# A GRU's input projection by Strassen's seven half products in place of eight, with the step loops written out

## The reference

```python
def cell(h, x):                        # 1024 steps in sequence, B = 4, D = 1024, float32
    gi = x @ W_ih + b_ih               # the projection: needs no h
    gh = h @ W_hh + b_hh               # the recurrence
    i_r, i_z, i_n = split(gi, 3); h_r, h_z, h_n = split(gh, 3)
    r = sigmoid(i_r + h_r); z = sigmoid(i_z + h_z)
    n = tanh(i_n + r * h_n)
    return (1 - z) * n + z * h
hs = scan(cell, cond, x)               # [4, 1024, 1024]
# mixture of experts on hs: the router takes x/|x| @ router_w, softmax, the best 2 of 8,
# their weights normalised
out = x + sum_e combine[:, e] * (hs @ Wa[e] @ Wb[e])     # rank 128
```

## Time and profile before

| what | value |
|---|---|
| median of 3 runs | 9792.21 us (9789.74 to 9792.78) |
| the profiled execution, its own time | 9795.94 us |
| its span, first to last instruction | 9794.1 us |
| mean granted TensorE clock | 0.998 |
| PE busy | 9705.0 us, 99% |
| DVE busy | 5534.7 us, 57% |
| ACT busy | 1224.2 us, 12% |
| POOL busy | 488.3 us, 5% |

### The profile page before, as it was taken

The page is one execution under the profiler, slowest core; times in us unless marked ns, Lnnn a source line. Parts: engine busy times, 40 slices in busy tenths (PEclk is TensorE's granted clock), DMA queues, the critical chain, the costliest instruction groups (busy, mean ns, idle before and its releaser), DMA issues.

```text
span 9794.1 us, 528922 instructions
## 1 busy us (share of the span) xinstructions
PE 9705.0 (99%) x230296; PEld 6479.3 (66%) x230296; DVE 5534.7 (57%) x29395; ACT 1224.2 (12%) x4788; POOL 488.3 (5%) x1142
## 2 busy tenths in 40 slices
PE   7999999999999999999999999999999999999999
PEld 4666666667666676666767666676676766767676
DVE  5555555555555555555555555555555555555664
ACT  2111111111111111111111111111111111111111
POOL 1000000000000000000000000000000000000100
PEclk9999999999999999999999999999999999999999
DMA  7121222212222122222222222222222222222343
GB/s 171 40 46 46 47 50 44 47 42 48 49 46 50 39 49 64 67 59 60 59 66 64 63 60 60 65 64 63 64 54 68 64 64 64 58 62 61 86 101 91
DMA packets 1421900, 603.63 MB, mean 62 GB/s; under 512 B 852816, under 2 KB 1373520, under 8 KB 1419536
## 3 DMA queue, kind: packets, MB, share of 16 engines
q1 hardware_dynamic: 1395216, 491.58, 21.6%
q0 software_dynamic: 24336, 77.98, 3.5%
HBM read 436.35 MB, written 159.72 MB: 61 GB/s over the span
## 4 chain that ended last, share of the span: by engine, by line
PE 97%; DVE 1%; DMA 1%; issue 0%; SPq 0%; ACT 0%; DVEq 0%
PE gh_ps L1114 80%; PE gi_ps L1136 13%; PE y_ps L1174 1%; PE y_ps L1187 1%; PE route_ps L1147 1%; DMA w_ih_tile<-in_L_cond_W_ih 1%; DVE gh L839 0%; PE gh_ps L1258 0%; PE gi_ps L1187 0%; PE gi_ps L1174 0%; DVE gh_sum L845 0%; SPq L353 0%; PE gi_ps L1244 0%; SPq L358 0%; ACT gate L1037 0%
## 5 line engine op out<-in xcount | busy, mean ns | idle before, releaser
L1114 PE MATMUL gh_ps<-w_hh_parts,h_parts 128*12 128x288 bf16 (+1 forms) x196608 | 8363.3, 326 | 33.3 <-DVE h_parts L890 13.5
L1114 PEld LDWEIGHTS gh_ps<-w_hh_parts,h_parts 128*12 128x12 bf16 x196608 | 5396.9, 88 | 2674.3 <-issue 98.4
L839 DVE STREAM_TRANSPOSE gh<-gh_ps 128x288 f32<-128x288 f32 (+1 forms) x2048 | 1193.3, 583 | 2525.9 <-PE gh_ps L1114 2522.5
L1136 PE MATMUL gi_ps<-x_t,w_ih_tile 128*32 128x256 f32 x24576 | 1682.9, 381 | 43.3 <-DMA w_ih_tile<-in_L_cond_W_ih 43.2
L1037 ACT ACTIVATE gate<-pre 128x24 f32<-128x24 f32 (+1 forms) x2048 | 471.1, 230 | 7303.1 <-DVE pre L852 7303.1
L1136 PEld LDWEIGHTS gi_ps<-x_t,w_ih_tile 128*32 128x32 f32 x24576 | 813.2, 111 | 561.4 <-DMA w_ih_tile<-in_L_cond_W_ih 48.6
L860 DVE TENSOR_TENSOR r_cand<-h_cand,gate 128x12 f32<-128x12 f32 (+1 forms) x2048 | 360.8, 176 | 603.6 <-ACT gate L1037 603.6
L845 DVE TENSOR_REDUCE gh_sum<-gh 128x36 f32<-128x108 f32 (+1 forms) x2048 | 651.0, 318 | 71.0
L872 DVE TENSOR_TENSOR zn<-one_minus_z,cand 128x12 f32<-128x12 f32 (+1 forms) x2048 | 360.0, 176 | 414.8 <-ACT cand L1040 398.7
L1040 ACT ACTIVATE cand<-cand_in 128x12 f32<-128x12 f32 (+1 forms) x2048 | 441.8, 216 | 1109.1 <-DVE cand_in L863 1109.1
L885 DVE TENSOR_TENSOR h_parts<-shared,h_parts 128x12 bf16<-128x12 f32 (+1 forms) x2048 | 358.8, 175 | 163.9 <-DVE shared L880 14.5
(11 more groups left out here) (140 smaller groups left out, 1823.0 us busy)
## 6 DMA issues: line engine op xcount, KB each, us to landing
w_ih_tile<-in_L_cond_W_ih SPq DMA_DIRECT2D x1544, 128.0 KB, 2.8
gi_scratch<-gi_stage SPq DMA_DIRECT2D x384, 128.0 KB, 2.3
gi<-gi_scratch SPq DMA_DIRECT2D x256, 192.0 KB, 4.4
shared<-wa_by_partition SPq DMA_DIRECT2D x58, 512.0 KB, 4.2
expert_b<-in_L_ffn_Wb SPq DMA_DIRECT2D x58, 512.0 KB, 3.5
x_raw<-expert_rows_of_h SPq DMA_DIRECT2D x228, 128.0 KB
x_raw<-in_x SPq DMA_DIRECT2D x272, 64.0 KB, 2.1
window_rows<-shared SPq DMA_DIRECT2D x124, 128.0 KB, 2.3
```

The source lines that it names most:

```text
L839: nc.vector.transpose(gh[k][:, :, :, :], ps[k][sp_][:, 0:GATES * n * Q].rearrange("p (q c i) -> p q c i", q=GATES, i=Q))\
L1114: ins = nc.tensor.matmul(ps[k_out][t % 2][j * Q:j * Q + SPLIT * B, 0:GATES * (o1 - o0) * Q], h_parts[:, (t - 1) % 2, c, :, :].rearrange("p ...
L1136: ins = nc.tensor.matmul(ps_i[m % 2][j * Q:(j + 1) * Q, 0:COLS], w_i[m % slots][:, c, j * Q:(j + 1) * Q], x_t[:, c, :, :].rearrange("p t b ...
```

## The change

W, a 2x2 matrix of halves for a pair of output columns (column m with m+12, input chunks 0 to 3 with 4 to 7), is multiplied with x, halved by chunks and by the block's time steps (32 and 32), in seven half products instead of eight. It is done for the projections of blocks 2 to 15, that is while blocks 1 to 14 are stepped. A half product has 4 chunks of 128x128 fp32: 4 quarters of a tile. There are 12 pairs x 7 products x 4 = 336 quarters a block. The order is p1, p6, p2, p5, p7, p3, p4, in two banks in turn, some added in PSUM onto what stands there.

- W's four sums are made by POOL while block 0 is stepped (`add_w`) and kept in DRAM beside W's own halves; SP then loads one half of 256 KB for each product (`load_half`, one DMA), into three buffers.
- Four sums of x are made by DVE at the end of step 0 of each block (`add_x`); the x of the next block but one is transposed in steps 62 and 63, after the gates.
- p1, p2 and p5 are copied out by ACT (`copy_product`), p6, p7 (two operations), p3 and p4 are added by DVE (`add_products`). Both stand behind both pieces of the step in which the product ended.
- A product's first quarter waits for what the product before the last one left behind in its bank or sum.
- The loops are written out; small tiles share memory (`r_cand` and `cand_in` are `h_cand`, the row buffer of the experts is `wa_x`, so `load_a` waits for `y_free` too).

```diff
+def quarter_schedule(steps, tiles):
+    rest = tiles - 3 - 5 * (steps - 3)
+    counts = [(0, 3)] + [(2 + (t * rest // (steps - 3) > (t - 1) * rest // (steps - 3)), 3) for t in range(1, steps - 2)]
+    counts += [(0, 0)] * 2
...
+PRODUCTS = ["p1", "p6", "p2", "p5", "p7", "p3", "p4"]
+BANK = [0, 1, 0, 1, 0, 1, 0]
+ADDS = [False, False, True, False, False, True, True]
...
+    PLAN_Q = quarter_schedule(TB, NPAIR * NP * (NC // 2))
...
+            def add_w(pair):        
...
+                tt(w_sum[0], a21, a22, ALU.add)
+                tt(w_sum[1], w_sum[0], a11, ALU.subtract)
+                tt(w_sum[2], a11, a21, ALU.subtract)
+                tt(w_sum[3], a12, w_sum[1], ALU.subtract)
+                pool.sem_inc(w_sum_ready, 1)
...
+            def add_x(f):
...
+                nc.vector.tensor_tensor(x_sum[0], b12, b11, ALU.subtract).then_inc(x_sum_ready, 1)
...
+                nc.vector.tensor_tensor(x_sum[1], b22, x_sum[0], ALU.subtract).then_inc(x_sum_ready, 1)
+                nc.vector.tensor_tensor(b12, b22, b12, ALU.subtract).then_inc(x_sum_ready, 1)
...
+                nc.vector.tensor_tensor(x_sum[2], b21, x_sum[1], ALU.subtract).then_inc(x_sum_ready, 1)
...
+            def add_products(f, q): 
...
+                dve.wait_ge(gi_done, done_before(f) + q + 1)
+                if what == "p6":
+                    dve.wait_ge(gi_copied, 3 * pair + 1)
+                    nc.vector.tensor_tensor(partial[:, :], bank, partial[:, :], ALU.add).then_inc(gi_summed, 1)
...
                     for half in range(2):
                         part(n, t, half)
...
+                    if n and not last:
+                        if t == 0:
+                            add_x(n + 1)
+                        for q in ended_products([*PLAN_Q[t][0], *PLAN_Q[t][1]]):
+                            add_products(n + 1, q)
...
-                with dve.Fori(lo, hi) as trip:
+                for trip in range(lo, hi):
...
                 for t in range(TB):
                     gates(n, t)
...
+                        for q in ended_products([*PLAN_Q[t][0], *PLAN_Q[t][1]]):
+                            copy_product(n + 1, q)
...
+            def project_products(tiles, f):
+                per = NC // 2
+                for i in tiles:
+                    q, c = i // per, i % per
+                    pair, s = pairs_before(f) + q // NP, q % NP
+                    what = PRODUCTS[s]
+                    if c == 0:
+                        pe.wait_ge(w_half_in[q % WH], ((f - 2) * (NPAIR * NP // WH) + q // WH + 1) * DMA)
+                        if q < 2:
+                            pe.wait_ge(xt_ready, f * NC + NC // 2)
+                        if q == 1:
+                            pe.wait_ge(x_sum_ready, (f - 1) * 4)
+                        if pair == 0 and s < 2:
+                            pe.wait_ge(gi_read, 2 * NM)
+                        elif s < 2:
+                            pe.wait_ge(gi_summed, 5 * (pair - 1) + 4 + s)
+                        elif what in ("p5", "p4"):
+                            pe.wait_ge(gi_summed, 5 * pair + (1 if what == "p5" else 2))
+                        else:
+                            pe.wait_ge(gi_copied, 3 * pair + {"p2": 1, "p7": 2, "p3": 3}[what])
+                    for j in range(NQ):
+                        ins = nc.tensor.matmul(
+                            ps_i[(pair + BANK[s]) % 2][j * Q:(j + 1) * Q, 0:COLS // 2],
+                            w_half[q % WH][:, c, j * Q:(j + 1) * Q],
+                            x_of[what][:, c, :, :].rearrange("p t b -> p (t b)"),
+                            start=(c == 0 and not ADDS[s]), stop=(c == per - 1),
+                            skip_group_check=ADDS[s])
```

More of the change, by code:

```diff
@@ L65 @@
 AT_REST = 20
+def quarter_schedule(steps, tiles):
+    rest = tiles - 3 - 5 * (steps - 3)
+    counts = [(0, 3)] + [(2 + (t * rest // (steps - 3) > (t - 1) * rest // (steps - 3)), 3) for t in range(1, steps - 2)]
+    counts += [(0, 0)] * 2
+    assert sum(a + b for a, b in counts) == tiles
+    at, plan = 0, []
+    for a, b in counts:
+        plan.append((range(at, at + a), range(at + a, at + a + b)))
+        at += a + b
+    return plan
+PRODUCTS = ["p1", "p6", "p2", "p5", "p7", "p3", "p4"]
+BANK = [0, 1, 0, 1, 0, 1, 0]
+ADDS = [False, False, True, False, False, True, True]
+NP = len(PRODUCTS)
 def tile_schedule(steps, tiles):
@@ L249, in recurrence @@
         w_i_in = [sem(f"w_ih_in{s}") for s in range(WR)]
+        w_half_in = [sem(f"w_half_in{s}") for s in range(WH)]
+        w_sum_ready = sem("w_sums_ready")
+        w_sum_out = sem("w_sums_out")
+        x_sum_ready = sem("x_sums_ready")
+        gi_copied = sem("gi_copied")
+        gi_summed = sem("gi_summed")
         gi_done = sem("gi_done")
@@ L318, in ended, with ended_products, column, done_before @@
             return [i // NC for i in tiles if i % NC == NC - 1]
+        def ended_products(tiles):
+            return [i // (NC // 2) for i in tiles if i % (NC // 2) == NC // 2 - 1]
+        def column(f, k):
+            return k if f == 0 else k // 2 + k % 2 * NPAIR
+        def done_before(f):
+            return min(f, 2) * NM + max(f - 2, 0) * (NPAIR * NP)
+        def pairs_before(f):
+            return (f - 2) * NPAIR
         def blocks_before(n):
@@ L476, in steps @@
                             load(k + i, i, s, *(set_of(k + i) if last else (0, k + i, k + i - 1)))
-                    if not last and t == X_LOAD:
+                    if n + 2 < NB and t == X_LOAD:
                         if experts:
@@ L726, in _ @@
                 for t in range(TB):
+                    for i in (*PLAN[t][0], *PLAN[t][1]):
+                        if n == 0 and i % (2 * NC) == 1:
+                            add_w(i // (2 * NC))
                     def due(at, v_last=FLUSH):
@@ L1073, in steps @@
                     gates(n, t)
[L1074 to L1078, removed]
+                    if n == 0:
+                        for k_ in ended([*PLAN[t][0], *PLAN[t][1]]):
+                            act.wait_ge(gi_done, done_before(1) + k_ + 1)
+                            act.wait_ge(gi_out[k_ % 2], (NM // 2 + k_ // 2) * DMA)
+                            evict(1, k_)
+                    elif not last:
+                        for q in ended_products([*PLAN_Q[t][0], *PLAN_Q[t][1]]):
+                            copy_product(n + 1, q)
                     if t in AT_RECORD:
@@ L1089, in _ @@
             for lo, hi, experts in PHASES:
-                with act.Fori(lo, hi) as trip:
+                for trip in range(lo, hi):
                     for s in range(TRIP):
@@ L1200, in steps, with project_next @@
                 for t in range(TB):
-                    tiles = ((), ()) if last else PLAN[t]
+                    tiles = ((), ()) if last else PLAN[t] if n == 0 else PLAN_Q[t]
+                    def project_next(some):
+                        if n == 0:
+                            project(some, 1, WL)
+                        else:
+                            project_products(some, n + 1)
                     pe.wait_ge(parts_ready[0], n * TB + (t + 1))
@@ L1223, in _ @@
             for lo, hi, experts in PHASES:
-                with pe.Fori(lo, hi) as trip:
+                for trip in range(lo, hi):
                     for s in range(TRIP):
```

209 lines of the change are left out of this document (161 added, 48 removed).

## The result

The changed kernel takes 10199.08 us (median of 4 runs, 10189.09 to 10204.4) against 9791.54 for the kernel before: a ratio of 1.0416, 95% interval 1.0403 to 1.0428. It is 407 us slower; 308 were forecast, and the measured time lies at the upper end of the range, 1 us inside it. The profiled execution took 10204.4 us, with a span of 10202.7 and a mean granted clock of 0.986 (0.998 before).

The account below looks back on a forecast made before the run. PE was taken to bound the kernel (97% of the chain of waits). From 9795.9: + 391 (waits) + 62 (clock) - 133 (fewer matmuls) - 12.5 (straight code) = 10103; the median lies 3.7 lower, so 10100 us, range 9990 to 10200.

Parts of the forecast that it names:

- The sign and the mechanism: Whole kernel: slower by 3.1%, because PE's waits for adds, copies and sums outweigh the saved matmuls; slower was given 92%.
- Waits within a step and over its edge: PE in blocks 1 to 14: 21.4 us a block within steps, 4.5 over edges, some 3.5 in blocks with experts.
- The seven steps: Each block's steps 7, 40, 48, 51 (waiting for DVE, 3.55 us each) and 18, 29, 59 (for ACT, 2.40 each).
- the clock times 8.87 and 7.72: Times in us after a step's products(t,1) start when PE goes on: 8.87 behind DVE's add, 7.72 behind ACT's copy.
- The clock: TensorE falling to half clock behind PE's long waits for DVE: 62 us, with bounds of 0 and 187.
- Two in three of the long waits: Of the 56 waits for DVE within a step, two in three charged with 1.67 us of half clock each.
- for the waits of 2.4 and 2.7 us ... 0: PE's waits for ACT's copies and the sums of x: no half clock behind them, 0 us.
- the first rival: The clock falls at every wait, short ones too: + 187 in place of + 62, 10225 us; chance 8%.
- POOL's sums: POOL's 48 sums of W in block 0: needed by PE 2.6 steps later, cost 0, at most 10 us.
- The sums of x: Step 1 of each block: p6's first quarter waits for DVE's four sums from step 0, 2.7 us a block.
- The saving: Projection in blocks 1 to 14: 336 quarters of 0.2175 us replace 192 tiles of 0.43, 9.5 us a block, 133 us.
- Straight code: Written-out loops remove three loop edges with their gaps and the half clock behind two of them: 12.5 us off.

Follow-up runs that it names:

- e4: Changed kernel with ACT's copies of products ending in the first slot ahead of the gates and DVE's adds of them ahead of its first piece; 9751.4 us, ratio 0.9952.
- e7: Changed kernel with PE doing unread bf16 matmuls ahead of each of the 98 waits within a step; 10113.69 us, ratio 1.0323.
- e6: Changed kernel with e4 and e5 together, sums of x halved behind steps 0 and 1, p6 waiting for two sums and starting in step 1's second slot; 9661.26 us.
- e1: Kernel before the change with its step loops written out and nothing else; 9775.58 us, ratio 0.9979.
- e2: Changed kernel with the six-quarter steps placed so that none begins with a product's last quarter; 9826.63 us, ratio 1.0031.
- e5: Changed kernel with W's 48 sums in block 0 made by DVE, two in a step behind piece 1, in place of POOL; 10175.09 us, ratio 1.0383.

## Why the prediction came out as it did

The sign and the mechanism were right. That the time lies inside the range is in part luck: the range was made for the clock and the edge waits, and POOL's 37 us were not in it. Step by step:

- **Waits within a step and over its edge**: 353 us were counted (391 less 14 x 2.7 for the sums of x). e4 took 448 away, of which e7 gives 85 to the clock: 363. Read directly, these waits are 306 us of idle time in 205 waits, and 347 with the 0.2 us before each in which the last matmuls ended. The seven steps were the right ones, and the clock times 8.87 and 7.72 came out as 8.83 in step 7 and, for ACT, 961.08 - 953.30 = 7.78. An add of 128x128 was put at 0.29 us and took 0.284.
- **The clock**: 62 us was the term, 107.7 the windows' sum. Two in three of the long waits was right (37 of 56), but some lost up to 2.9 us for the 1.67 taken, 73 us together. The step that failed is "for the waits of 2.4 and 2.7 us ... 0": 21 of 56 of them were followed by half clock, 35 us. The rule of the Trainium skill (TensorE: Matmul & The Clock Gate, the section on how HAM oscillation bites in real kernels) that waits between bursts of matmuls bring the clock down each time anew is borne out in part: the granted clock fell behind 58 of the 112 waits and not behind 54, and taken in full the rule gives the 187 us of the first rival, for 108 measured.
- **POOL's sums**: "cost 0, at most 10 us for the whole block" is the step that was wrong outright: 37 us. I looked only at who waits for the sums, not at what else they hold up. The Trainium skill (SBUF — State Buffer, SBUF: two separate sides) says that a GpSimd operation and a VectorE operation in a two-port mode take the same pair of ports, as do a GpSimd operation that reads SBUF and a VectorE operation with two SBUF inputs, and that one of them is blocked in full until the other ends. The trace agrees as far as it goes: L980 and L992 have two SBUF inputs, and so have all the other lengthened operations but L985, a TENSOR_SCALAR, and once L929, a CAST, whose modes the trace does not show.
- **The sums of x**: 2.7 us a block; PE's waits of 2.4 to 2.7, with 0.2 us before them in which the matmuls ended. From e4 to e6 90 us went; less block 0's 37, 53 are left for them with their clock, 38 + 17 = 55 by the terms.
- **The saving**: 133 us, of which e6 less e1 shows 114. The block without experts took 587.4 us in e1 and 579.1 in e6 by the start of its logits, 8.3 us less and not 9.5; with 14 blocks that is the difference. It is not the quarter's price: from start to start three quarters take 0.655 us in e6 and two tiles 0.863 in e1, so a quarter is 0.218 and a tile 0.432, which give 9.5 again. The missing 1.2 us a block lie around them: all matmuls of the projection take 73.7 to 75.6 us of a block where the quarters' price makes 73.4, and the recurrence's take up to 0.9 us more than in e1 (0.7 less in one of four blocks read). Why stays open.
- **Straight code**: 12.5 us, measured 19 against its own before and 16 against the median shown. The term's own parts (9.57 of gaps and 3.3 of half clock, less 0.9) make 12.0, not 12.5.

Added from the runs: 363 + 85 + 37 + 53 - 114 - 19 = 405, of 407. This sum must close but for the choice of 19 or 16, since the steps from after to e4, e6, e1 and before make up the whole; it does not confirm how 448 and 90 are divided, which rests on e7 and on block 0's 37. The forecast was 99 us short. By the same runs 38 of these are the clock and the sums of x taken together (85 + 53 measured, 62 + 38 forecast), 37 POOL, 19 the saving and 10 the waits, less 6 for straight code: 98.

## What to carry to other kernels

When work is moved into gaps, put each release where its producer's engine can do it first, not at the end of a step: here the same copies and adds cost 448 us behind both pieces, and ahead of them PE waits for none. A schedule of uneven steps has to be checked for each phase in which producer and consumer fall, since seven of 82 consumers made nearly all the loss (372 of 407 us, by e2). A side engine's work is not free because nobody waits for it: look at what it shares.

## What the runs showed of the hardware that I had not expected

- TensorE's clock fell to 0.50 (1.2 GHz) behind waits as short as 2.2 us, though only behind 11 of 42 such waits, and behind 37 of 56 of 3.3 us or more. In block 0 it fell once behind a wait of 2.06 us (at 214.99) and not behind one of 2.46 (at 671.83). What sets one wait apart from the next in the same step of another block stays open. Filling 2.1 of 3.3 us with idle products brought it to none of 56.
- A wait of 3.3 us could cost 2.9 us more by the clock (step 7 of block 1), so the clock can nearly double a wait's price.
- DVE operations of 0.17 us ran to 1.26 beside POOL additions of 1.27 us; those that read PSUM did not: the transpose L959 kept its 0.48 us beside one at 264.34, and so in all nine places of block 0 where it stands beside one (0.68 us for its larger form). The TENSOR_REDUCE L965, which has one SBUF input, kept its time in eleven.
- The same kernel's median moved by 6 us between chips, and two profiles with the same waits, the changed kernel's and e5's, differ by some 10 us in half clock alone.
